# LoRA-A of gate and up in the free columns of the last feature tile, and x's first chunk in two pieces

## The reference

```python
# 1. gated FFN with one LoRA adapter (rank 16) for each of the 8 batch rows
def lora_add(base, inp, A, B):
    Ab, Bb = A[lora_indices], B[lora_indices]
    t = einsum('bri,bni->bnr', Ab, inp)
    return base + einsum('bor,bnr->bno', Bb, t) * 0.5
gate = lora_add(x @ W_gate.T, x, A_gate, B_gate)     # 1376 features
up   = lora_add(x @ W_up.T,   x, A_up,   B_up)
act  = silu(gate) * up
h = lora_add(act @ W_down.T, act, A_down, B_down)    # 512
# 2. x = x + h @ W.T + bias + lora(h)   3. a conditional linear layer with a +-1 mask for each row
# 4. x = x + top-16 of 64 rank-16 experts
```

## Time and profile before

| | |
|---|---|
| median of 3 runs | 361.28 us (361.18 to 361.67) |
| profiled execution, its own time | 359.89 us |
| its span | 358.2 us |
| granted clock of PE, mean | 1.00 |

### The profile page before, as it was taken

The page is one execution under the profiler, slowest core; times in us unless marked ns, Lnnn a source line. Parts: engine busy times, 40 slices in busy tenths (PEclk is TensorE's granted clock), DMA queues, the critical chain, the costliest instruction groups (busy, mean ns, idle before and its releaser), DMA issues.

```text
span 358.2 us, 4760 instructions
## 1 busy us (share of the span) xinstructions
PE 354.3 (99%) x1728; PEld 299.2 (84%) x1728; DVE 197.6 (55%) x303; ACT 141.2 (39%) x191; POOL 83.2 (23%) x89
## 2 busy tenths in 40 slices
PE   8999999999999999999999999999999999999996
PEld 7888888888888888988888898888888888888886
DVE  3758664245434533576574476769888868511101
ACT  5567444234423432434662552547363353201100
POOL 1738886644240001100000000000032054002200
PEclk9999999999999999999999999999999999999999
DMA  7855542333130041579317209201042012101011
GB/s 253 274 167 168 176 133 62 113 102 88 53 108 0 0 171 47 164 276 345 96 48 214 93 2 354 116 5 53 3 158 77 2 59 73 47 29 59 31 59 59
DMA packets 14979, 38.86 MB, mean 108 GB/s; under 512 B 2305, under 2 KB 4097, under 8 KB 13681
## 3 DMA queue, kind: packets, MB, share of 16 engines
q1 hardware_dynamic: 11728, 31.24, 25.8%
q0 software_dynamic: 2656, 6.95, 6.6%
q10 hardware_dynamic: 576, 0.43, 0.4%
HBM read 36.51 MB, written 2.10 MB: 108 GB/s over the span
## 4 chain that ended last, share of the span: by engine, by line
PE 99%; DVE 0%; issue 0%
PE ps L1052 28%; PE ps L1053 28%; PE ps L1054 28%; PE ps L1174 3%; PE ps L1072 3%; PE ps L1080 1%; PE ps L1087 1%; PE ps L1103 1%; PE ps L1091 1%; PE ps L1095 1%; PE ps L1264 1%; PE ps L1251 1%; PE ps L1273 0%; PE ps L1282 0%; DVE x L1045 0%; DVE warm L746 0%
## 5 line engine op out<-in xcount | busy, mean ns | idle before, releaser
L1052 PE MATMUL ps<-x_hl,w_hl 128*128 128x512 f32 x160 | 62.8, 392 | 0.0
L1053 PE MATMUL ps<-x_hl,w_hl 128*128 128x512 f32 x160 | 62.7, 392 | 0.0
L1054 PE MATMUL ps<-x_hl,w_hl 128*128 128x512 f32 x160 | 62.3, 389 | 0.0
L383 POOL DMA_INDIRECT b_raw<-b_gu,row_of x36 | 36.1, 1003 | 34.7 <-DVE b_st L713 25.4
L421 POOL TENSOR_TENSOR am_hl<-am_raw,am_hl 128x512 fp32r<-128x512 f32 x8 | 11.1, 1392 | 136.8 <-ACT am_hl L438 136.8
L734 DVE TENSOR_TENSOR glu<-glu,ps 128x512 f32<-128x512 f32 x22 | 15.0, 685 | 37.6 <-PE ps L1072 37.6
L1054 PEld LDWEIGHTS ps<-x_hl,w_hl 128*128 128x128 f32 x160 | 30.1, 188 | 6.5
L438 ACT ACTIVATE act<-glu 128x512 f32 (+1 forms) x22 | 13.8, 632 | 54.3 <-DVE glu L734 54.2
L1052 PEld LDWEIGHTS ps<-x_hl,w_hl 128*128 128x128 f32 x160 | 30.1, 188 | 5.2
L1053 PEld LDWEIGHTS ps<-x_hl,w_hl 128*128 128x128 f32 x160 | 30.2, 189 | 4.8
L1053 PE MATMUL ps<-act,wd_hl 128*128 128x512 f32 x80 | 31.1, 389 | 0.0
(11 more groups left out here) (139 smaller groups left out, 700.6 us busy)
## 6 DMA issues: line engine op xcount, KB each, us to landing
wc_raw<-mask_w SPq DMA_DIRECT2D x8, 1024.0 KB, 7.4
w_raw<-w_gu SPq DMA_DIRECT2D x9, 512.0 KB, 3.4
wd_raw<-w_dn SPq DMA_DIRECT2D x10, 256.0 KB, 3.0
x_raw<-x_t SPq DMA_DIRECT2D x8, 256.0 KB, 5.3
w_raw<-w_t SPq DMA_DIRECT2D x2, 1024.0 KB, 6.9
x<-x_t SPq DMA_DIRECT2D x2, 1024.0 KB, 6.1
am_raw<-a_moe SPq DMA_DIRECT2D x8, 256.0 KB, 2.7
bm_raw<-b_moe SPq DMA_DIRECT2D x4, 512.0 KB, 3.8
```

Of the source, the lines that this page charges most:

```text
L383: nc.gpsimd.indirect_dma_start(b_raw[f % 2][:, p].rearrange("q m f -> q (m f)"), None, b_gu, bass.IndirectOffsetOnAxis(ap=row_of[:, f - 2, ...
L1052: nc.tensor.matmul(out, w_high, m_high, start=start, stop=False)
L1053: nc.tensor.matmul(out, w_high, m_low, start=False, stop=False)
L1054: return nc.tensor.matmul(out, w_low, m_high, start=False, stop=stop)
```

## The change

The 11th tile (LAST) has 96 features, and its other 32 columns now hold LoRA-A's weights: 16 ranks each for the two batch rows of a pair. Since A is another one in each pair, `w_last` holds the tile four times, once a pair, and its matmuls have 256 columns (`project_last`): 2 halves x 2 projections x 2 pairs x 4 chunks x 3. Output rows 96 to 127 are t, rows 0 to 95 the tile's features. `lora_down` and `a_st` go. The tile runs third: its first half after the first half of tiles 0 and 1, its second half after the first six adapts. `t_mask` reads rows 96 to 127, `t_high` makes two copies a half, `t_low` one subtraction; LoRA-B needs 96 rows and one low part (`b_low`, one operation of 32x1024). Evictions are numbered by FIRST_EVICTED, in banks FIRST_BANK. x's first chunk arrives, is split and is multiplied (for tile 0) in two pieces of 256 tokens; tile 1's first chunk of w is issued by SP behind them; the warm-ups are 7 for 10. Two things follow in the queues: SP issues the last tile's w and LoRA-A before x's second half, and POOL's gather of LoRA-B (now three tiles, a pair at a time) starts ahead of its LoRA-A.

```diff
-WARM_UP = 10
+WARM_UP = 7
+LAST = FT - 1
+FIRST_EVICTED = ((0, 0), (1, 0), (LAST, 0), (LAST, 1), (0, 1), (1, 1))
+FIRST_BANK = (4, 0, 2, 4, 6, 0)
...
 # SP
-            load_x0(0)
+            for h in range(2):
+                sp.dma_start(x_raw[:, 0, h * PAIR:h * PAIR + PAIR],
+                             x_t[:, 0, h * PAIR:h * PAIR + PAIR]).then_inc(dma_x0_pair[h], 16)
+            sp.dma_start(w_raw[1][:, 0], w_gu[1, :, 0]).then_inc(dma_w_first[1][0], 16)
             load_x0(1)
...
-            for k in range(KD):
-                sp.dma_start(x_raw[:, k, HALF:T], x_t[:, k, HALF:T]).then_inc(dma_x1[k], 16)
+            sp.dma_start(w_last_raw[:], w_gu[LAST]).then_inc(dma_w_last, 16)
             sp.wait_ge(dma_small, 16)
             for b in range(A_BY_SP):
...
+            for k in range(KD):
+                sp.dma_start(x_raw[:, k, HALF:T], x_t[:, k, HALF:T]).then_inc(dma_x1[k], 16)
             sp.dma_start(const_sb[:], consts).then_inc(dma_const, 16)
...
 # POOL
-            load_b_first()
-            for f in range(2, FT):
-                pool.wait_ge(b_hi, f - 1)
-                pool.wait_ge(b_lo, 2 * f - 2)
+            load_b_first(0)
+            for b in range(A_BY_SP, BATCH):
...
+            load_b_first(1)
+            for f in range(2, LAST):
+                if f < 4:
+                    pool.wait_ge(bf_lo, 3 * f - 3)
+                else:
+                    pool.wait_ge(b_hi, f - 3)
+                    pool.wait_ge(b_lo, f - 3)
                 load_b(f)
                 if f == AD_LOADS_AFTER:
+                    pool.wait_ge(up_ready, evicted(LAST, 1) + 1)
                     load_ad()
...
 # ACT
             def b_high(f, slot, use):
                 act_e.wait_ge(dma_b[slot], 16 * NPAIR * (use - 1))
                 if isinstance(f, int) and f == 2:
-                    act_e.wait_ge(up_ready, 3)
-                copy(b_st[slot][:], b_raw[slot][:]).then_inc(b_hi, 1)
+                    act_e.wait_ge(up_ready, evicted(0, 1) + 1)
+                copy(b_st[slot][0:F_LAST], b_raw[slot][0:F_LAST]).then_inc(b_hi, 1)
...
+            def first_silu(n):
+                if n >= 2:
+                    act_e.wait_ge(act_lo, n - 1)
+                silu(n, n % 2, FIRST_BANK[n], first_rows(n))
...
             x_high(3, 0)
-            for k in range(2):
-                x_high(k, 1)
-            act_e.wait_ge(dma_a, 16 * A_BY_SP)
...
+            for p in range(2):
+                w_last_high(p)
+            a_high(0)
+            for k in range(KD):
                 x_high(k, 1)
...
+                for rows in (slice(0, 32), slice(64, 96)):
+                    copy(t_st[rows, two], t_raw[0:32, two]).then_inc(t_hi, 1)
...
+            b_first_high(0)
+            for p in range(2, NPAIR):
+                w_last_high(p)
+            a_high(1)
             t_high(0)
+            b_first_high(1)
+            first_silu(0)
+            first_silu(1)
+            first_act_high(0)
+            first_act_high(1)
+            first_silu(2)
+            first_act_high(2)
             w_high(2, 0, 2)
...
             t_high(1)
...
-            act_e.wait_ge(act_lo, 1)
-            silu(2, 0, 2)
+            for n in range(3, 5):
+                first_silu(n)
+                first_act_high(n)
             b_high(2, 0, 2)
-            act_e.wait_ge(act_lo, 2)
-            silu(3, 1, 6)
-            for u in range(2):
-                act_high(2 + u, u, u, 1)
+            first_silu(5)
+            first_act_high(5)
...
 # DVE
+            b_first_low(0)
+            for p in range(2, NPAIR):
+                w_last_low(p, p + 3)
+            a_low(1, 7)
             dve.wait_ge(dma_const, 16)
...
             t_mask(0)
+            t_low(0)
...
+            for n in range(3, 5):
+                first_gate(n)
+                first_act_low(n)
             b_low(2, 0)
...
 # PE
-            def lora_down(p):
...
+            def project_last(s):
+                bank = FIRST_BANK[2 + s]
+                pe.wait_ge(wl_hi, 4 * s + 4)
+                pe.wait_ge(wl_lo, 4 * s + 4)
+                for m in range(2):
+                    if s == 1:
+                        pe.wait_ge(glu_done if m else silu_done, 1)
+                    for p in (2 * s, 2 * s + 1):
+                        cols = slice(p * PAIR, p * PAIR + PAIR)
+                        for k in range(KD):
+                            last = mm3(ps[:, bank + m, PAIR * (p % 2):PAIR * (p % 2) + PAIR],
+                                       w_last[:, p, 0, k, m], w_last[:, p, 1, k, m],
+                                       x_hl[:, 0, k, cols], x_hl[:, 1, k, cols],
+                                       k == 0 and p % 2 == 0, k == KD - 1 and p % 2 == 1)
                 last.then_inc(t_ready, 1)
...
+            for h in range(2):
+                project_pair(h)
+            project_first(1, 0)
+            for k in range(1, KD):
                 for u in range(2):
                     project_first(u, k)
...
+            project_last(0)
             for k in range(KD):
                 for m in range(2):
-                    last = project(0, 0, m, 1, first=True, part=range(k, k + 1))
+                    last = project(0, FIRST_BANK[4] + m, 1, first=True, part=range(k, k + 1))
             last.then_inc(w0_used, 1)
...
+            for n in range(3):
+                adapt_first(n)
+            project_last(1)
             for m in range(2):
-                pe.wait_ge(t_masked, m + 1)
-                project(1, 1, m, 1)
-            adapt_first(1)
+                pe.wait_ge(glu_done if m else silu_done, 2)
+                project(1, FIRST_BANK[5] + m, 1)
...
+            for n in range(3, 6):
+                adapt_first(n)
...
                 if s == 0:
-                    pe.wait_ge(b_hi, f + 1)
-                    pe.wait_ge(b_lo, 2 * f + 2)
+                    pe.wait_ge(b_hi, f - 1)
+                    pe.wait_ge(b_lo, f - 1)
```

More of the change, by code:

```diff
@@ L753, in _ @@
             nc.vector.tensor_copy(w_hl[0][:, 0, 0:1], w_raw[0][:, 0:1]).then_inc(w_hi, 1)
[L754 to L757, removed]
+            for h in range(2):
+                pair = slice(h * PAIR, h * PAIR + PAIR)
+                dve.wait_ge(x_hi if h else x_pair_hi, 1)
+                low(x_hl[:, 1, 0, pair], x_raw[:, 0, pair], x_hl[:, 0, 0, pair]).then_inc(x_lo if h else x_pair_lo, 1)
+                w_first_low(h, slice(0, 1), h + 1)
+            x_low(1, 0)
+            for u in range(2):
+                w_first_low(u, slice(1, 2), 3 + u)
             x_low(2, 0)
@@ L761, in _, with w_last_low @@
             x_low(3, 0)
-            for k in range(2):
-                x_low(k, 1)
[L764 to L774, removed]
+            def w_last_low(p, n):
+                dve.wait_ge(wl_hi, n)
+                low(w_last_own(p, 1), w_last_raw[:, :, :, 0:F_LAST], w_last_own(p, 0)).then_inc(wl_lo, 1)
@@ new lines, in a_low, with b_first_low @@
+            def a_low(g, n):
+                for par in range(2):
+                    dve.wait_ge(wl_hi, n + par)
+                    low(a_part(1, g, par), a_own(g, par), a_part(0, g, par)).then_inc(wl_lo, 1)
+            for p in range(2):
+                w_last_low(p, p + 1)
+            a_low(0, 3)
+            for k in range(KD):
+                x_low(k, 1)
+            def b_first_low(g):
+                two, rows = slice(2 * g, 2 * g + 2), slice(64, 96)
+                for u, stack in enumerate((b_st[0], b_st[1], b_last)):
+                    dve.wait_ge(bf_hi, 3 * g + u + 1)
+                    low(stack[rows, two], b_first[rows, two, u], stack[rows, two]).then_inc(bf_lo, 1)
@@ L791, in _ @@
             b_first_low(1)
-            t_low(0)
+            first_gate(0)
+            first_gate(1)
+            first_act_low(0)
+            first_act_low(1)
+            first_gate(2)
+            first_act_low(2)
             w_low(2, 0)
             t_mask(1)
-            for u in range(2):
-                gate(u, u, 4 * u + 1)
             t_low(1)
-            for u in range(2):
-                act_low(u, u, u, 0)
-            gate(2, 0, 3)
+            for n in range(3, 5):
+                first_gate(n)
+                first_act_low(n)
@@ L801, in _ @@
             b_low(2, 0)
-            gate(3, 1, 7)
-            for u in range(2):
-                act_low(2 + u, u, u, 1)
-            with dve.Fori(0, (FT - 3) // 2) as i:
+            first_gate(5)
+            first_act_low(5)
+            with dve.Fori(0, (FT - 5) // 2) as i:
                 for u in range(2):
@@ L809, in _ @@
                     evacuate(2 * i + 2 + u, u)
+            w_low(FT - 2, 1)
+            b_low(FT - 2, 1)
+            evacuate(FT - 3, 0)
             dve.wait_ge(dma_lora, 32)
@@ L1057, in halves, with project @@
                 return slice(s * HALF, s * HALF + HALF)
-            def project(slot, bank, m, s, first=False, part=range(KD)):
+            def project(slot, bank, s, first=False, part=range(KD)):
```

(20 more changed lines are left out.)

274 lines of the change are left out of this document (144 added, 130 removed).

## The result

The changed kernel takes 365.82 us (median of 6 runs, 364.18 to 366.94) where the kernel before takes 361.38 (6 runs, 361.18 to 361.67): ratio 1.012, 95% interval 1.010 to 1.0141. It is 4.4 us slower; the forecast was 1.1 us faster. The two profiled executions lie further apart: before, 359.89 us (span 358.2), 1.5 us under its median; after, 366.39 us (span 364.7), 0.6 over.

A forecast was written before the change was run, and what follows sets the result against it. PE, 99% of busy time and chain, was taken as the bound. Terms -3.82 + 0.51 - 0.39 + 2.63 = -1.07 us took 361.28 to 360.2, with a range of 357.5 to 361.5.

The forecast's parts named there:

- Cover for project_last(0): At 16.3 us: w_last and four rows of LoRA-A ready by 15.1, 1.2 us spare, so 0 cost.
- The rival with 7%: After the warm-ups or the stall, PE's clock drops to 1.2 GHz: 363.2 us, slower; 7% chance.
- one output (3.0 us): Slow-clock price in tile 2: 13 lengths of a 512-wide matmul, each 0.228 us more.
- Late data: Before the first adapts: x's second half lands at 19.3, PE waits 1.2 us, 361.4 in all; 15% chance.
- The wait for B of tile 2: At tile 2's adapt: b_low is ready at T+6.80 against PE's T+4.17, a wait of +2.63 us.
- The last tile in 256 columns: In the moved last tile: 96 matmuls of 256 columns replace 48 of 512, +0.51 us.
- LoRA-A's matmuls: In two stretches, the first 16.69 to 18.60: 32 matmuls of 256 columns removed, -3.82 us.
- The start: First halves of tiles 0 and 1: tile 1's first chunk lands sooner, block runs earlier, -0.39 us.
- The sum without waits: Whole kernel with b_low in time at tile 2: -3.70 us, 357.6; a rival with 14% chance.

The follow-up runs named there:

- e1: The changed kernel with POOL's three LoRA-A loads first and its LoRA-B gather started only when w_last has landed: 366.16 us, ratio 1.0151.
- e8: The changed kernel with POOL's three LoRA-A loads ahead of its gather, but no wait for w_last: 366.28 us, one execution.
- e7: The kernel before with POOL's gather of LoRA-B (first two of four) ahead of its three LoRA-A loads: 361.24 us, one execution.
- e11: The kernel before with one useless 512 KB DMA on SP at w_last's place: 361.40 us, one execution.
- e4: The changed kernel with 7 matmuls on zeros between the first halves of tiles 0 and 1 and w_last's: 367.10 us, ratio 1.0165.
- e9: e3 plus w_last's splits for pairs 2 and 3 before x's second half, t_mask before LoRA-B's low parts, t_high(0) before a_high(1): 358.03 us, ratio 0.9909.
- e2: The changed kernel with B of tile 2 split earlier, b_high directly behind the fourth eviction's silu, b_low behind its multiply: 361.79 us, ratio 1.0029.
- e6: The kernel before with the start's edits alone (x's first chunk in two pieces, tile 1's first w chunk on SP, seven warm-ups): 365.26 us, ratio 1.0074.
- e10: e9 with the kernel before's start (x's first chunk whole, tile 1's first w chunk on ACT's queue, ten warm-ups): 358.19 us, ratio 0.9908.
- e3: The changed kernel with both the edits of e1 and e2: 360.82 us, ratio 0.9997.

## Why the prediction was wrong

**The step that failed** is "Cover for project_last(0)", with its "1.2 us spare, 0". I took LoRA-A's flight from its median of 3.4 us, under the DMA load of the kernel before; even there the longest was 4.9, which would have eaten the 1.2 us. The change itself altered that load: w_last's 512 KB and a gather that starts 5.7 us sooner. I had named both moves in the diff and costed neither as a load on the engines that LoRA-A's DMAs share. The flight became 7.7 us, and the cover turned into +3.35. e1 and e8 take the wait away by POOL's order alone (the gather behind its LoRA-A loads); e7 and e11 show each load by itself, some 2 us of landing each.

**The second failure is the clock.** The rival with 7% came true twice, for 1.59 and 1.54 us. My argument against it was that the clock reads 1.00 in the idle first 1.18 us, "which ran straight into full speed". That reading was wrong. The same two-instruction matmul on zeros costs 0.42 us in the warm-up (14 instructions in 3.36) and 0.25 in e4 (14 in 1.72): the warm-ups ran slowly, and the column shows nothing of it. I set the price at one output (3.0 us) for one fall; two falls of 1.6 came out near that, which is luck: each was half of it. The step of that sum, 0.228 more for a 512-wide matmul, is 0.20 in the trace (0.43 apart for 0.228). The Trainium skill's rule (TensorE: Matmul & The Clock Gate, What's actually happening: half rate is the default, activity lifts it) agrees with these rows: slow warm-ups at the start, and 0.50 behind waits of 3.2 and 2.5 us. Over all traces the clock fell behind the ten waits of 3.2, 3.0, 2.8, 2.5 (six times) and 1.8 us, and not behind those of 2.4, 1.9 and 1.4 us and less: a wait's length alone doesn't decide it, since 1.8 brought a fall and 2.4 none.

**Late data**, the rival with 15%, was too narrow. x's second half flew 9.0 to 9.4 us, beyond the 6.2 that I called the longest. In the changed kernel that cost only 0.11 us, since PE was late too. Late t is what kept e1, e4 and e8 as slow as the changed kernel, and there the order on DVE and ACT made it late: t was masked behind the splits of x's second half, of LoRA-B (landed at 21.7 in e1) and of w_last. With LoRA-B at 21.3, e9 has no wait there, by order alone.

**What held.** The wait for B of tile 2: predicted +2.63, measured +2.63 between reaching that adapt and its start, with T at 45.92 and b_high from 50.28 to 51.32, where I had T+4.35 to T+5.40; e2 removes it by order alone. The last tile in 256 columns: +0.51 predicted, +0.60 measured. LoRA-A's matmuls: -3.82. The start: -0.39 predicted, -0.38 measured, but by luck, since steps that I had wrong cancelled. w's first tile was cast at 3.84 and not 4.65, so PE went on at 4.22 and not 5.05; the 12 matmuls of 256 columns then took 2.4 us, 0.20 each and not 0.12, close to the 0.21 of the stretches at 0.50; and tile 1's first chunk was copied by 6.22 and not 5.9. e6 and e10 show besides that this read one place and not the whole. The sum without waits, 357.6, is nearly what e9 reaches (358.03, with 1.4 us of waiting left in its profile). So the saving was there, and the price was the order of queues around it.

## What to carry to other kernels

- A cover worked out from a transfer's median flight holds only for the load of that trace. When a change moves or adds transfers in the same stretch, price them first: here 0.5 MB or a gather moved up by 5.4 us made LoRA-A's DMAs land 2 us later each, in a stretch whose DMA share was already 0.83.
- Where PE is the bound, look along every chain that feeds it, for the wait behind the first wait: e1 removed the longest wait and gained nothing, because another took its place; e2 removed one with no other behind it and gained 4.0 us; the full saving came in e9, when the chain of t was free as well. Order each engine's queue by when PE needs the result, and put what waits for a transfer behind what doesn't.
- Add the clock to the price of a stall of PE: where it fell behind waits of 3.2 and 2.5 us, each fall cost 1.5 to 1.6 us more. It fell behind a wait of 1.8 us and not behind one of 2.4, so count it as a risk and not as a rule.

## What the runs showed that I had not expected

- The granted clock's column reads 1.00 while the warm-ups run at about half speed (0.42 against 0.25 us a matmul, above). It is no evidence of full speed at a kernel's start. The 12 real matmuls behind the changed kernel's seven warm-ups were slow too (0.20 us each for 256 columns), under the same 1.00.
- Two DMAs of 128 KB for one of 256 KB at the head of SP's queue, with one more behind them, moved LoRA-A's first issue by 1.8 us (7.68 to 9.47) in e6. Two issues of 0.43 are half of that; for the rest, later issues on the queue took up to 1.16 us instead of 0.61.
- The same kernel doesn't lose its clock each time. The mean clock was 0.995 or less in seven of e2's ten executions, in nine of e3's ten and in eight of e6's 11, and 0.999 or 1.00 in all of e9's four and e10's six. A single trace of a kernel with a stall shows one of these cases.
